# Variances of two layer normalisations moved from VectorE's statistics instructions to ScalarE squares with an accumulated sum, with every engine's order rewritten

## The reference, cut to what matters

```python
x = L0_attn_out                                    # (8, 512, 256), float32
x = layernorm(x + attn(x))                         # attn(x) = x + alpha * (reads @ W_read.T)
x = layernorm(x + ffn(x))                          # ffn: FP4-quantised gate, up, down; silu(gate) * up

def layernorm(x, eps=1e-5):
    m = mean(x, -1); v = var(x, -1)
    return (x - m) / sqrt(v + eps)
```

## Time and profile before

| | |
|---|---|
| median of 3 runs | 349.37 us (349.29 to 349.79) |
| the profiled execution | 349.22 us |
| its span, first to last instruction | 347.5 us |
| PE busy | 314.8 us (91%) |
| DVE busy | 319.5 us (92%) |
| ACT busy | 178.7 us (51%) |
| POOL busy | 242.8 us (70%) |
| mean granted PE clock | 0.985 |

### The profile page before, as it was taken

One profiled execution on the slowest core, in us unless ns is written; L12 is line 12 of the kernel. 1 busy time (PEld: TensorE's weight loads), 2 busy tenths in 40 slices (PEclk: granted clock), 3 DMA queues, 4 the chain that ended last, 5 costly groups with the idle time before them and its releaser, 6 DMA issues.

```text
span 347.5 us, 7092 instructions
## 1 busy us (share of the span) xinstructions
PE 314.8 (91%) x2234; PEld 305.2 (88%) x2234; DVE 319.5 (92%) x806; ACT 178.7 (51%) x378; POOL 242.8 (70%) x261
## 2 busy tenths in 40 slices
PE   0595787989999999999999999999999999999883
PEld 0384777979999999999999999999999999999883
DVE  1789898999999999999999999999999999999994
ACT  3534454644555555535554556554555445545453
POOL 1579595675767668967787678668785785676653
PEclk9987899999999999999999999999999999999999
DMA  5810300030002200040003100210020000000002
GB/s 178 262 51 3 121 0 0 3 121 4 0 17 75 80 17 15 16 138 17 0 15 116 50 0 15 91 60 16 16 78 2 15 15 17 18 15 3 30 31 77
DMA packets 13611, 15.61 MB, mean 45 GB/s; under 512 B 1168, under 2 KB 11280, under 8 KB 13584
## 3 DMA queue, kind: packets, MB, share of 16 engines
q1 hardware_dynamic: 13296, 15.27, 13.4%
q10 hardware_dynamic: 288, 0.00, 0.0%
HBM read 11.08 MB, written 4.19 MB: 44 GB/s over the span
## 4 chain that ended last, share of the span: by engine, by line
PE 53%; DVE 30%; issue 9%; POOL 2%; DMA 2%; ACT 2%; SPq 1%; DVEq 0%; POOLq 0%; ACTq 0%
PE bank L1529 9%; PE bank L1531 9%; PE bank L1530 9%; PE gu L1529 7%; PE gu L1530 7%; PE gu L1531 7%; DVE h_y L928 4%; PE bank L1603 4%; DVE h_g L933 3%; DVE h_am L1054 3%; DVE w_raw L1047 3%; DVE hqT_lo L1075 2%; DMA w_raw<-in_L_ffn_w_up_dram 2%; DVE pr L975 1%; DVE h_rs L923 1%
## 5 line engine op out<-in xcount | busy, mean ns | idle before, releaser
L1529 PE MATMUL gu<-guT_hi,xqT_hi 128*128 128x352 f32 x256 | 85.0, 332 | 1.0 <-DVE w_raw L1047 0.9
L1530 PE MATMUL gu<-guT_lo,xqT_hi 128*128 128x352 f32 x256 | 82.9, 324 | 0.0
L1531 PE MATMUL gu<-guT_hi,xqT_lo 128*128 128x352 f32 x256 | 82.8, 323 | 0.0
L403 POOL TENSOR_TENSOR h_q<-h_g,h_ns 128x704 f32<-128x704 f32 x32 | 46.2, 1443 | 34.3 <-DVE h_g L933 34.3
L1529 PEld LDWEIGHTS gu<-guT_hi,xqT_hi 128*128 128x128 f32 x256 | 48.2, 188 | 2.1 <-DVE w_raw L1047 1.3
L632 ACT ACTIVATE w_raw<-gu 128x352 f32<-128x352 f32 x64 | 29.6, 462 | 37.5 <-PE gu L1531 37.3
L1530 PEld LDWEIGHTS gu<-guT_lo,xqT_hi 128*128 128x128 f32 x256 | 48.2, 188 | 0.0
L1531 PEld LDWEIGHTS gu<-guT_hi,xqT_lo 128*128 128x128 f32 x256 | 48.0, 188 | 0.0
L396 POOL TENSOR_TENSOR h_n<-w_raw,h_rs 128x704 f32<-128x704 f32 x32 | 44.6, 1393 | 4.1 <-DVE h_rs L923 4.0
L1530 PE MATMUL bank<-dnT_lo,hqT_hi 128*128 128x256 f32 x160 | 45.2, 282 | 0.0
L1531 PE MATMUL bank<-dnT_hi,hqT_lo 128*128 128x256 f32 x160 | 45.2, 282 | 0.0
(11 more groups left out here) (111 smaller groups left out, 900.4 us busy)
## 6 DMA issues: line engine op xcount, KB each, us to landing
x_full<-attn_out_transposed_dram SPq DMA_DIRECT2D x8, 512.0 KB, 4.2
xs<-in_L_attn_out_dram SPq DMA_DIRECT2D x8, 512.0 KB, 3.5
out_dram<-wq_gu SPq DMA_DIRECT2D x32, 128.0 KB, 1.7
w_raw<-in_L_ffn_w_down_dram SPq DMA_DIRECT2D x1, 704.0 KB, 9.1
w_raw<-in_L_ffn_w_gate_dram SPq DMA_DIRECT2D x1, 640.0 KB, 7.0
w_raw<-in_L_ffn_w_up_dram SPq DMA_DIRECT2D x1, 640.0 KB, 7.9
wrT<-n_W_read_transposed_dram SPq DMA_DIRECT2D x1, 256.0 KB, 6.2
ww<-in_L_attn_W_write_dram SPq DMA_DIRECT2D x1, 256.0 KB, 7.8
```

Source lines behind the costliest of these rows:

```text
L403: nc.gpsimd.tensor_tensor(blocks(h_q[:, p, 0:I]), blocks(h_g[:, p, :]), per_block(h_ns[:, p, :], HB), ALU.mult).then_inc(h_quant, 1)
L1529: nc.tensor.matmul(dst, lh, rh, start=(first and i == 0), stop=False)
L1530: nc.tensor.matmul(dst, lh, rl, start=False, stop=False)
L1531: last = nc.tensor.matmul(dst, ll, rh, start=False, stop=(i == len(terms) - 1))
```

## The change

- `x_stats` and `out_stats` are gone, and with them all 64 `bn_stats`, all 64 `bn_aggr` and the no-operation ahead of each.
- `x_residual` writes each of its two tiles by an instruction of its own, of 256 columns, and both `x_residual` and `out_residual` also give the sum of each row (`accum_out`).
- ACT has `x_deviations` (two activations) and `out_deviations` (one): the square of (sum - 256 z), with the sum as bias and an accumulated sum of the squares. The squares themselves go to new tiles `z_off` and `o_off` that nothing reads.
- `x_moments` and `out_moments` keep two small `tensor_scalar`, and now wait for ACT.
- The lists of all five engines are reordered, most products change banks, and the conditions on which PE may reuse a bank change with them. `combine` now fills `bank[3]`, so that the first `scores` no longer wait for its reader.

```diff
             def x_residual(n, u, reused=True):
...
-                nc.vector.scalar_tensor_tensor(
-                    z[:, 2 * u:2 * u + 2, :].rearrange("p i d -> p (i d)"),
-                    xs[:, 2 * u:2 * u + 2, :].rearrange("p i d -> p (i d)"), 2.0, r_bank[u][:], ALU.mult,
-                    ALU.add).then_inc(z_ready, 1)
-
-            def x_stats(n, u):
-                dve.wait_ge(z_ready, 2 * n + u + 1)
-                for i in (2 * u, 2 * u + 1):
-                    nc.vector.bn_stats(z_bn[:, i, :], z[:, i, :]).then_inc(z_stats, 1)
+                for q in range(2):
+                    i = 2 * u + q
+                    last = nc.vector.scalar_tensor_tensor(z[:, i, :], xs[:, i, :], 2.0, r_bank[u][:, q * D:(q + 1) * D],
+                                                          ALU.mult, ALU.add, accum_out=z_sum[:, i:i + 1])
+                last.then_inc(z_ready, 1)
...
-                for i in (2 * u, 2 * u + 1):
-                    dve.wait_ge(z_stats, 4 * n + i + 1)
-                    nc.vector.nop(nofuse=True)
-                    nc.vector.bn_aggr(z_mv[:, i, :], z_bn[:, i, :]).then_inc(z_moments, 1)
...
+                dve.wait_ge(z_dev, 2 * n + u + 1)
+                nc.vector.tensor_scalar(z_nm[:, c], z_sum[:, c], -1.0 / D, None, ALU.mult)
+                nc.vector.tensor_scalar(z_ve[:, c], z_ssq[:, c], 1.0 / D ** 3, LN_EPS, ALU.mult,
+                                        ALU.add).then_inc(z_var, 1)
...
+            def x_deviations(n, u):
+
+                act.wait_ge(z_ready, 2 * n + u + 1)
+                for i in (2 * u, 2 * u + 1):
+                    last = nc.scalar.activation(z_off[:, i, :], z[:, i, :], ACT.Square, bias=z_sum[:, i:i + 1],
+                                                scale=-float(D), accum_out=z_ssq[:, i:i + 1])
+                last.then_inc(z_dev, 1)
...
+            def out_deviations(k, p):
+                act.wait_ge(o_ready, k + 1)
+                nc.scalar.activation(o_off[:, p, :], o_z[:, p, :], ACT.Square, bias=o_sum[:, p:p + 1], scale=-float(D),
+                                     accum_out=o_ssq[:, p:p + 1]).then_inc(o_dev, 1)
...
-                nc.vector.tensor_tensor(o_z[:, t % 2, :], x1[:, par, t, :], d_bank[t][:, 0:D],
-                                        ALU.add).then_inc(o_ready, 1)
+                p = t % 2
+                nc.vector.scalar_tensor_tensor(o_z[:, p, :], d_bank[t][:, 0:D], 1.0, x1[:, par, t, :], ALU.mult, ALU.add,
+                                               accum_out=o_sum[:, p:p + 1]).then_inc(o_ready, 1)
```

```diff
 # DVE, start
             w_maxima(2)
-            scale_comb()
+            w_maxima(3)
             w_reciprocals(1)
             w_to_grid(0)
+            scale_comb()
+            w_magic_add(1)
+            w_to_grid(1)
             rest_comb()
+            w_divisors(2)
             dve.wait_ge(mask_ready, 1)
             decay_scores(0, 0, reused=False)
 # PE, start
             combine([])
-            scores(0, 0, [(comb_ready, 1)])
+            scores(0, 0, [])
 # PE, body: its end, and then its beginning
+                gate_up(k + 1, b, 1, 0)
+                reads(n, 0, [(v_lo_ready, 2 * n + 1)])
+                gate_up(k + 1, b, 1, 1)
+                scores(n - 1, 3, [(hT_lo_ready, 8 * n - 19)])
+                xq_transpose(n - 2, 1, [(z_ready, 2 * n - 1)])
+                h_transpose(k - 6, 2, 1, [(hT_lo_ready, 2 * k - 12)])
+                values(n - 1, 1, [(o_ready, 4 * n - 10)])
+                h_transpose(k - 5, 3, 0, [(xqT_lo_ready, 2 * n - 2)])
+                gate_up(k - 2, b - 1, 2, 0)
 # ACT, body: its beginning
+                x_deviations(n - 1, 0)
                 gate_silu(k - 3, 1, 0)
 # DVE, body: its end
+                x_residual(n, 0)
                 h_to_grid(k - 1, 1)
+                hidden(k + 1, 1, 0)
                 h_reciprocals(k, 0)
+                x_moments(n, 0)
 # PE, end
             gate_up(31, 7, 3, 0)
-            down(26, 2, [(xqT_lo_ready, 16)])
+            h_transpose(27, 3, 1, [(hT_lo_ready, 54)])
             gate_up(31, 7, 3, 1)
+            down(26, 2, [(hT_lo_ready, 53)])
 # DVE, end
             hidden(31, 1, 1)
             h_maxima(31, 1)
             h_divisors(31, 1)
             h_reciprocals(31, 1)
+            out_residual(26, 0, 2)
+            h_rest(28, 0, 0)
             h_rest(28, 0, 1)
+            h_magic_add(30, 0)
+            h_to_grid(30, 0)
+            h_magic_add(31, 1)
```

More of the change, by code:

```diff
@@ L1337, in _ @@
+            h_reciprocals(21, 1)
+            out_residual(18, 0, 2)
             h_to_grid(20, 0)
-            decay_scores(6, 3)
-            x_residual(6, 0)
-            x_stats(6, 0)
-            h_reciprocals(21, 1)
-            x_moments(6, 0)
-            v_rest(6, 1)
-            hidden(22, 0, 0)
-            hidden(22, 0, 1)
+            x_magic_add(6, 0)
+            out_moments(18, 0)
+            h_rest(19, 3, 1)
+            x_residual(6, 1)
+            x_to_grid(6, 0)
             h_maxima(22, 0)
+            h_rest(20, 0, 0)
@@ new lines, in _ @@
+            x_divisors(7, 0)
+            x_reciprocals(7, 0)
+            h_maxima(25, 1)
+            h_rest(22, 2, 1)
+            h_divisors(25, 1)
+            h_to_grid(24, 0)
+            hidden(26, 0, 0)
+            v_rest(7, 1)
+            h_reciprocals(25, 1)
+            hidden(26, 0, 1)
+            x_magic_add(7, 0)
+            out_moments(21, 1)
+            x_to_grid(7, 0)
+            out_residual(22, 1, 2)
+            h_maxima(26, 0)
+            x_residual(7, 1)
+            h_divisors(26, 0)
@@ L1691, in _ @@
-            scores(2, 2, [(xqT_lo_ready, 3)])
             gate_up(4, 1, 0, 0)
+            h_transpose(1, 1, 0, [(xqT_lo_ready, 3)])
+            values(2, 0, [(o_ready, 1)])
             gate_up(4, 1, 0, 1)
-            h_transpose(2, 2, 0, [(pr_ready, 10)])
+            h_transpose(1, 1, 1, [(pr_ready, 10)])
+            reads(2, 0, [(v_lo_ready, 5)])
+            h_transpose(2, 2, 0, [(hT_lo_ready, 3)])
+            down(1, 1, [(pr_ready, 11)])
             gate_up(5, 1, 1, 0)
-            h_transpose(2, 2, 1, [(v_lo_ready, 5)])
@@ L1697, in _ @@
             gate_up(5, 1, 1, 1)
-            xq_transpose(1, 1, [(pr_ready, 11)])
-            values(2, 1, [(hT_lo_ready, 5)])
-            scores(2, 3, [(o_ready, 2)])
-            reads(2, 0, [(xqT_lo_ready, 4)])
-            gate_up(6, 1, 2, 0)
-            gate_up(6, 1, 2, 1)
             def body(b, par):
                 k, n = b * 4, b + 1
-                h_transpose(k - 5, 3, 0, [(v_lo_ready, 2 * n)])
-                down(k - 6, 2, [(z_ready, 2 * n - 1)])
+                scores(n - 1, 3, [(hT_lo_ready, 8 * n - 19)])
@@ L1734, in body @@
-                reads(n, 0, [(xqT_lo_ready, 2 * n)])
-                gate_up(k + 2, b, 2, 0)
-                gate_up(k + 2, b, 2, 1)
-            run(pe, body)
-            down(18, 2, [(z_ready, 13)])
-            h_transpose(19, 3, 0, [(v_lo_ready, 14)])
+            run(pe, body)
+            h_transpose(18, 2, 1, [(hT_lo_ready, 36)])
+            xq_transpose(5, 1, [(z_ready, 13)])
+            scores(6, 3, [(hT_lo_ready, 37)])
+            values(6, 1, [(o_ready, 18)])
+            h_transpose(19, 3, 0, [(xqT_lo_ready, 12)])
@@ L1741, in _ @@
+            gate_up(22, 5, 2, 0)
+            gate_up(22, 5, 2, 1)
+            down(18, 2, [(pr_ready, 28)])
             h_transpose(19, 3, 1, [(hT_lo_ready, 38)])
-            reads(6, 1, [(pr_ready, 28)])
-            h_transpose(20, 0, 0, [(hT_lo_ready, 39)])
+            reads(6, 1, [(v_lo_ready, 14)])
             gate_up(23, 5, 3, 0)
+            h_transpose(20, 0, 0, [(z_ready, 14)])
             down(19, 3, [(hT_lo_ready, 40)])
-            scores(7, 0, [(z_ready, 14)])
-            h_transpose(20, 0, 1, [(o_ready, 19)])
@@ L1761, in _ @@
+            reads(7, 0, [(v_lo_ready, 15)])
+            down(21, 1, [(pr_ready, 31)])
+            xq_transpose(6, 1, [(z_ready, 15)])
+            scores(7, 3, [(hT_lo_ready, 45)])
+            h_transpose(22, 2, 1, [(hT_lo_ready, 44)])
             gate_up(25, 6, 1, 1)
-            h_transpose(22, 2, 1, [(v_lo_ready, 15)])
-            down(21, 1, [(hT_lo_ready, 44)])
-            reads(7, 0, [(xqT_lo_ready, 14)])
-            values(7, 1, [(hT_lo_ready, 45)])
+            values(7, 1, [(o_ready, 22)])
```

1011 lines of the change are left out of this document (486 added, 525 removed).

## The result

The changed kernel takes 339.75 us (median of 4 runs, 339.18 to 340.35), against 349.58 us (349.29 to 350.66) for the kernel before on the same chip: a ratio of 0.9713, 95% interval 0.9683 to 0.9744. The forecast was 341.5, with a range of 337.5 to 347.0 and an own range of 339 to 344 for the likeliest case. The profiled span went from 347.5 to 337.4 us.

The account below looks back on a forecast made before the run. The start was taken as DVE's work plus hand-offs, the loop as PE's, the end as nearly both. From 349.2 us, 4.5 at the start and 3.5 at the end left 341.2, stated as 341.5; range 337.5 to 347.0.

Parts of the forecast that it names:

- the split of the start's 4.5 us: Start: 2.0 us net from lighter DVE work plus 2.5 us of DVE idle time filled by the new order.
- In the loop, nowhere: Loop: DVE's relief gains nothing, as PE doesn't wait for DVE; same length expected from about 94 to 263 us.
- Rival (d): Loop: slower, a late square holds ACT's silu and so PE, once per batch in six batches; 351 to 356; chance 0.08.
- my dear end for the relief: DVE: if each sum's read also emptied the pipeline, the relief would be nearer to 2 us per batch.
- the 1.48 us of the earlier trace: Start: a DVE idle time of 1.48 us, to be filled by rounding of weight slice 1.
- The cap by PE's loss: End: relief of 7.0 us exceeds the 4.3 us PE loses, which caps the gain; 3.5 us taken, bounds 0.5 and 5.
- The last tile: Last tile: statistics to POOL's start took 1.04 us, now 1.0 to 1.3; no change taken, bound +0.3.
- The loads: SP's loads move past each other by one place and cost nothing, each issued well ahead of its use.
- (a): Start and end give much less, as moments wait for ACT's in-order list; 345 to 348; chance 0.24 for 344 to 348.6.
- (b): All goes better: idle times filled, PE at full clock from 25 us, 7 and 5 us gained; 337; chance 0.13 below 339.
- (c): Relief off the path, PE the pacer from end to end, order a draw: 349 within 0.7; chance 0.03.

Follow-up runs that it names:

- run 1: Kernel before with the changed kernel's lists and banks but the old statistics, bn_stats right ahead of bn_aggr: 371.64 us.
- run 2: Kernel before with the new lists and banks and the old statistics, each bn_stats one call behind its residual: 365.72 us.
- run 3: Kernel before with its own lists and banks, but the new operations, squares put into ACT's old list where the residuals ended: 348.36 us.
- run 6: Changed kernel, DVE redoing the removed statistics of the output tiles only, in the loop, into tiles nothing reads: 348.20 us.
- runs 5 and 6: Changed kernel with removed statistics redone on DVE in the loop, results unread: all of them 354.33 us, output tiles' only 348.20 us.
- run 10: Changed kernel with five steps moved earlier in the start, on DVE's and ACT's lists, to fill idle time: 339.64 us.
- run 9: Changed kernel with each square on ACT made twice, the first into a tile nobody reads: 353.66 us.
- run 11: Changed kernel with the loop's x_residual(n - 1, 1) four calls earlier and the mean z_nm of two row tiles one column at a time: 340.98 us.
- run 12: Changed kernel with both small operations of x_moments made one column at a time, nothing else moved: 338.88 us.

## Why the prediction was right, and where its reasons weren't

**The total and its terms.** Forecast: 4.5 us from the start, 3.5 from the end, nothing from the loop. The cut traces say 4.5 and 3.7 at the ends, and 1.9 in the middle. The sizes were right at both ends, the end's in part because 0.7 us of its work moved into the middle. The 1.9 us is what was missing from 341.5 to 339.75. Most of it, 1.55 us, came from the first and the last of the five batches, where the lists change over; 0.55 us of that is a PE wait for `hidden` at 275.25 us that is gone. What gives the rest is not shown.

**The step that failed: the split of the start's 4.5 us, 2.0 from relief and 2.5 from the order, as two terms that add up.** The order alone gives 0.1 us in the start (run 1; 0.9 us lost in run 2), the operations alone give 0.0 (run 3), the two together 4.5; the spread of about a microsecond changes nothing in that. The end is the same in kind: 0.8 alone (run 3), a loss of 2.4 or a gain of 0.4 (runs 1 and 2), 3.7 together. In the old lists the relief opens idle time on DVE where it stands, as PE waits for steps that are placed late; in the new lists the queue is too long for its places without the relief. The numbers show that the two need each other; this account of why is read from the waits and is not tested by a run. I had bounded each term by itself, and no bound held the product.

**"In the loop, nowhere".** For the old order that is right, and run 3 shows it: 3.65 us less on DVE and the same batch. For the new order it is wrong. Its lists have DVE wait 3.7 us per batch where the old had it wait 0.6, and that is paid for with the relief: without it the batch takes 41.17 to 41.90 us (runs 1 and 2), and with 1.66 us of load 39.13 (run 6). The forecast of the loop came out because relief and new waits cancel, which is luck: PE needs the 37.1 us, and by the cover of 0.6 to 1.0 us in runs 5 and 6 DVE's queue needs an estimated 36.1 to 36.5 of them. The price of the reorder in the loop, about 4 us per batch without the operations, was in no term of my sum. Rival (d) had a loss per batch in it, but by a late square, which is another way.

**The costs of the operations.** DVE's relief was 3.1 us of busy time per batch against my 3.3. The size is right by luck. The accumulated sum, which I priced at 0.07 us each, costs about 0.01 by its starts, and in run 3 the relief is 3.65 us. In the changed kernel's batch 0.5 us of that is lost again, as other instructions of DVE step longer in the new order (the four `h_g` 3.45 us for 3.22, the eight `hidden` 3.60 for 3.41). The Trainium skill, "VectorE: DVE Perf Modes", section "Two Vector instructions with no wait between them", has it right that such an operation is two instructions: 64 rows of a read are there, of 84 ns by the median. That each could also empty the pipeline, my dear end for the relief, did not happen: the next residual starts with the read, at 29.69. ACT's share was 3.8 us per batch against 4.8 to 6.4: a square 0.40 to 0.41 by starts and its read 0.09 or so, where I had taken whole durations that overlap.

**The start's idle times.** I had the 1.48 us of the earlier trace rows filled by the rounding of a weight slice. DVE is idle 1.44 us there in the changed kernel as well (at 19.50, for ACT's square of that slice), while `rest_comb` stands behind it. So the sum held though this entry of it did not. What went are PE's waits at 44.6, 58.6 and 76.33 us, shows the last; run 10 says why a single wait is a poor guide there.

**The end.** The cap by PE's loss held (3.7 of 4.3), though the 4.3 us was a reckoning by the loop's pace: PE's waits over 0.15 us in that stretch of the kernel before add up to 2.9. **The last tile** took 5.4 us from the start of PE's last instruction in place of 5.5, no change as forecast. **The loads** moved past each other cost nothing that any trace shows.

**The rivals.** (a), the waits in order for ACT, did not come: DVE waits 0.2 and 1.1 us in the whole span for the squares. But it was close, as run 9 shows: half a microsecond more of ACT per square, and 14 us are gone, more than the gain. I had called ACT's throughput covered; the throughput is, and it is the wrong measure. (d), a silu late in the new loop, is seen in its mild form, 1.1 us per batch of DVE waiting for it, within the 37.1 us. (b) and (c) did not come.

## What to carry to other kernels

An engine's idle time is slack only if the waits in it shrink when work is added: here DVE was not busy for 4.2 of 37.1 us, and 1.66 us of load, with 0.98 us of a collision that the load brought about, cost 2.0. Put a known dead load on an engine, in one stage, to measure its slack, before you call a stage another engine's.

When lists that run in order are rewritten together with lighter operations, the two are one change. Price the new order with the old durations too; a sum of a term for each can be right by luck.

## What the runs showed of the hardware

**Instructions that wait for GpSimd.** Which engine of the two is stretched depends on who starts first: `x_y`, two operands from SBUF, takes 0.68 us in the changed kernel, where it starts ahead, and 1.67 us in run 6, where it starts behind (above). A small instruction can be caught as well. In the changed kernel one `z_nm` over two columns took 1.35 us, from 31.78 to 33.13, and POOL's multiplication of 704 columns ended at 33.11. In run 11 the mean, by single columns, took 0.2 us for both at that place, and the 2-column `z_ve` behind it took 1.22 us, until 34.20; POOL's operation ended at 34.18:

```profile
32.21 1.97 POOL L355 TENSOR_TENSOR wq_gu<-h_g,h_ns 128x704 f32<-128x704 f32 x1 [0.83 <-DVE h_g L977]
```

```profile
32.86 0.20 DVE L1047 TENSOR_SCALAR z_nm<-z_sum 128x1 f32<-128x1 f32 x2
32.98 1.22 DVE L1048 TENSOR_SCALAR z_ve<-z_ssq 128x2 f32<-128x2 f32 x1
```

In run 12 no one of 64 single-column instructions is over 0.154 us, though the four of that place start between 32.8 and 33.1 us, inside a POOL operation of 32.17 to 34.14. In all fourteen traces no single-column `TENSOR_SCALAR` is over 0.156 us. The Trainium skill, "SBUF — State Buffer", section "Who interferes with whom", says that an operation of DVE with two SBUF inputs contends with a GpSimd instruction that reads SBUF, and so does one in a two-port mode, which a `tensor_scalar` can enter: whoever issues first gets the shared pair of ports for the whole instruction, and the other is fully blocked. The traces agree (1.80 us for GpSimd's operation behind `x_y`, 1.67 us for `x_y` behind GpSimd's), and they add that two columns of float32 are enough to be caught, while one column never was.

**Sums for next to nothing on DVE, cheap on ACT.** In the changed kernel the read of an accumulated sum costs about 0.01 us by starts on DVE (rows of 84 ns) and about 0.09 on ACT, where a square follows it at once (126.47 to 126.57 us; rows of 192 ns).
